# Decoder slots of a four-stage megakernel: scan tail, centring product, squares and mean in two halves of 256 columns

## The reference, cut to what matters

```python
h = jnp.einsum('blv,dv->bld', x, Win) + bin            # x: (32, 64, 512), D = 64
def body(h, p):                                        # 4 layers
    y = silu(layernorm(h, l1w, l1b))                   # first norm
    y = sconv(y, pr + 1j*pi, lr + 1j*li)               # complex exponential filter along time
    h = h + y * scl
    y = layernorm(h, l2w, l2b)                         # second norm
    y = silu(jnp.einsum('bld,fd->blf', y, w1) + b1_)   # F = 256
    y = jnp.einsum('blf,df->bld', y, w2) + b2_
    return (h + y, None)
...
x = _layernorm(x + attn(x)); x = _layernorm(x + xattn(x, ctx, ctx)); x = _layernorm(x + ffn(x))
```

## Time and profile before

| | us |
|---|---|
| median of 3 runs | 315.83 |
| the runs | 313.68, 315.85, 315.83 |
| time of the profiled execution | 316.37 |
| span of the profiled execution | 314.4 |

### The profile page before, as it was taken

How to read it: one execution, slowest core, us unless ns; L and a number is a source line. 1 busy time by engine, 2 the same in 40 slices (tenths; PEclk the granted TensorE clock), 3 DMA queues, 4 the chain that set the end, 5 groups by cost and what they waited for, 6 DMA issues and landing times.

```text
span 314.4 us, 4410 instructions
## 1 busy us (share of the span) xinstructions
PE 271.2 (86%) x1051; PEld 109.0 (35%) x1058; DVE 267.8 (85%) x871; ACT 234.2 (74%) x540; POOL 152.5 (48%) x195
## 2 busy tenths in 40 slices
PE   1587789889898898798999999999999999879762
PEld 1223123223222232244454443544534444423220
DVE  5979799898898987339999999999999999996580
ACT  7046579798898898897478867889788897775642
POOL 1026424014023121302237766787778988899731
PEclk9999799999999999999999999999999999997978
DMA  6999989802021300610000101001112101211141
GB/s 196 394 243 342 379 161 197 180 34 57 11 69 33 133 0 0 111 24 2 3 0 0 18 17 20 18 15 37 51 51 50 40 25 40 53 51 50 50 151 67
DMA packets 22575, 26.52 MB, mean 84 GB/s; under 512 B 10771, under 2 KB 11411, under 8 KB 22550
## 3 DMA queue, kind: packets, MB, share of 16 engines
q1 hardware_dynamic: 20470, 22.06, 22.9%
q0 software_dynamic: 2080, 4.19, 7.9%
HBM read 15.89 MB, written 4.19 MB: 64 GB/s over the span
## 4 chain that ended last, share of the span: by engine, by line
PE 35%; DVE 27%; issue 15%; ACT 14%; DMA 4%; POOL 2%; SPq 1%; POOLq 0%; DVEq 0%; ACTq 0%
PE ps L443 4%; DMA big<-in_xT_dram 4%; DVE ps L1171 4%; PE ps L495 4%; PE ps L469 3%; PE ps L477 3%; PE ps L488 3%; DVE X L1103 3%; DVE big L1183 2%; PE ps L417 2%; PE ps L393 2%; PE ps L430 2%; PE ps L564 2%; ACT L754 2%; DVE ps L1077 2%
## 5 line engine op out<-in xcount | busy, mean ns | idle before, releaser
L1103 DVE SCALAR_TENSOR_TENSOR X<-ps,X 128x512 f32<-128x512 f32 x48 | 32.0, 681 | 11.6 <-PE ps L417 6.3
L651 ACT ACTIVATE big<-X,lnv 128x512 f32<-128x512 f32 x48 | 34.3, 714 | 8.8 <-DVE X L1103 8.7
L393 PE MATMUL ps<-ctx_ring,consts 64*128 64x512 f32 (+1 forms) x96 | 36.5, 659 | 0.0
L443 PEld LDWEIGHTS ps<-consts,big 96*128 96x128 f32 x256 | 29.8, 191 | 13.0 <-issue 10.6
L443 PE MATMUL ps<-consts,big 96*128 96x64 f32 x256 | 32.0, 278 | 0.7 <-DVE big L1138 0.7
L1183 DVE TENSOR_TENSOR big<-ps,ctxf 128x512 f32<-128x512 f32 x48 | 30.3, 682 | 1.3 <-PE ps L477 0.7
L679 ACT ACTIVATE X<-X,lnv 128x512 f32<-128x512 f32 x32 | 25.9, 808 | 0.6
L1171 DVE MATCH_REPLACE8 ps<-m,big 128x64 f32<-128x64 f32 x128 | 25.2, 215 | 0.0
L722 ACT ACTIVATE big<-ps 128x512 f32<-128x512 f32 x16 | 9.5, 596 | 20.9 <-PE ps L457 20.9
L841 POOL TENSOR_TENSOR big<-big 128x512 f32<-128x512 f32 x4 | 5.8, 1444 | 36.0 <-DVE big L1250 26.0
L488 PE MATMUL ps<-big,consts 128*128 128x512 f32 x32 | 17.1, 615 | 5.0 <-DVE qs L1078 4.9
(11 more groups left out here) (185 smaller groups left out, 643.9 us busy)
## 6 DMA issues: line engine op xcount, KB each, us to landing
big<-in_xT_dram SPq DMA_DIRECT2D x4, 1024.0 KB, 9.1
ctx_ring<-in_ctx_dram SPq DMA_DIRECT2D x16, 256.0 KB, 4.2
out_dram<-X SPq DMA_DIRECT2D x16, 256.0 KB, 2.2
X<-in_x_dram SPq DMA_DIRECT2D x2, 1536.0 KB, 11.6
X<-rows_sb POOLq DMA_DIRECT2D x1, 3072.0 KB, 21.7
X<-in_wq_dram SPq DMA_DIRECT2D x1, 1024.0 KB, 5.7
X<-in_x_dram SPq DMA_DIRECT2D x2, 512.0 KB, 4.0
X<-rows_sb POOLq DMA_DIRECT2D x1, 1024.0 KB, 8.6
```

What stands on the lines that cost most here:

```text
L393: mm(bank(LANE_BANK[lane]), mat((CY_0, CY_1, CY_C)[f])[half, :], ctx_ring[half, r * N:(r + 1) * N], start=True, stop=True).then_inc(s_cfor ...
L443: last = mm(ps[:, 2 * N + j * P + b * L:2 * N + j * P + (b + 1) * L], PQ[0:EVEN, b * N + j * P:b * N + (j + 1) * P], mat(IC_E)[0:EVEN, 0:L ...
L651: squared[k, n] = chain(a(JUNK[k], row(n), ACT.Square, bias=st[:, 0:1], scale=-float(V), accum_out=st[:, 2:3]))
L1103: stt(row(m), bank(b), 0.0, row(m), ALU.add, ALU.add, accum_out=st[:, 0:1]).then_inc(s_sum[k], 1)
```

## The change

Three things change, all inside the slots.

1. The tail of the recurrence on DVE: instead of one table product over 1024 columns and one sum over 512, there are for each half h (4 of the 8 sequences, 256 columns of `U1` and of `U2`) a table product over 2 x 256 columns and a sum over 256. Each sum raises `s_scan`.
2. The centring product on PE, the squares of set o on ACT and the variance product of set o on PE are each issued as two instructions of 256 columns. The centring product of half h waits for sum h; both halves of the squares wait for both centring products (`s_xc` at 2m); the variance product of half h waits for the squares of half h; the logarithm that follows waits for both.
3. Order. On ACT the two squares now stand between the logarithm and the exponential of set s, and the second context copy stands before that logarithm. On PE the context form that stood behind the centring product now stands at the slot's beginning, ahead of the variance product of set s.

The core of the diff:

```diff
                 if second:
+                    context_rest(2 * m - 1)
                     pe.wait_ge(s_sq1, m + 1)
                     mm(bank(0), mat(MEAN), SQ[s], start=True, stop=True).then_inc(s_var1, 1)
-                    pe.wait_ge(s_scan, m)
-                    mm(XC[o], mat(CENTER), U1, start=False, stop=False, skip_group_check=True).then_inc(s_xc, 1)
-                    context_rest(2 * m - 1)
+                    for h in range(2):
+                        pe.wait_ge(s_scan, 2 * m - 1 + h)
+                        mm(XC[o][:, half(h)], mat(CENTER), U1[:, half(h)], start=False, stop=False,
+                           skip_group_check=True).then_inc(s_xc, 1)
                     if m == 1:
                         pe.wait_ge(s_b1sum, 1)
-                    pe.wait_ge(s_sq2, m)
-                    mm(bank(2), mat(MEAN), SQ[o], start=True, stop=True).then_inc(s_var2, 1)
+                    for h in range(2):
+                        pe.wait_ge(s_sq2, 2 * m - 1 + h)
+                        last = mm(bank(2)[:, half(h)], mat(MEAN), SQ[o][:, half(h)], start=True, stop=True)
+                    last.then_inc(s_var2, 1)
...
                 if second:
                     context_copied(act, copy, 2 * m - 1, 0)
+                    context_copied(act, copy, 2 * m - 1, 2)
                 act.wait_ge(s_var1, m + 1)
-                chain.then_wait(a(RS[s], bank(0), ACT.Ln, bias=eps[:, :]))
+                logarithm = chain(a(RS[s], bank(0), ACT.Ln, bias=eps[:, :]))
+                if second:
+                    for h in range(2):
+                        act.wait_ge(s_xc, 2 * m)
+                        a(SQ[o][:, half(h)], XC[o][:, half(h)], ACT.Square, bias=base[:, l:l + 1]).then_inc(s_sq2, 1)
+                chain.wait(logarithm)
                 a(RS[s], RS[s], ACT.Exp, scale=-0.5).then_inc(s_rs1, 1)
                 if second:
-                    act.wait_ge(s_xc, m)
-                    a(SQ[o], XC[o], ACT.Square, bias=base[:, l:l + 1]).then_inc(s_sq2, 1)
-                    context_copied(act, copy, 2 * m - 1, 2)
                     act.wait_ge(s_var2, m)
...
-                    do(tt(US, US, tables(l, T_COSG, L), ALU.mult))
-                    tt(U1, U1, U2, ALU.add).then_inc(s_scan, 1)
+                    for h in range(2):
+                        part_of = slice(h * SEQ // 4, (h + 1) * SEQ // 4)
+                        do(tt(US[:, :, part_of, :], US[:, :, part_of, :], half_tables(l, T_COSG, L), ALU.mult))
+                        c = half(h)
+                        tt(U1[:, c], U1[:, c], U2[:, c], ALU.add).then_inc(s_scan, 1)
```

More of the change, by code:

```diff
@@ L282, in stats, with half @@
             return lnv[:, (SETS * k + n % SETS) * 8:(SETS * k + n % SETS + 1) * 8]
+        def half(h):
+            return slice(h * N // 2, (h + 1) * N // 2)
         def here(n):
@@ L1097, in tables, with half_tables @@
                         .broadcast_to([P, 2, SEQ // 2, n]))
+            def half_tables(l, at, n):
+                at += l * T_LEN
+                return (tab[:, at:at + 2 * n].rearrange("p (v t) -> p v t", v=2).unsqueeze(2)
+                        .broadcast_to([P, 2, SEQ // 4, n]))
             VS, US = (piece(k, 2).rearrange("p (v s t) -> p v s t", v=2, t=L) for k in (4, 6))
```

## The result

The changed kernel takes 320.1 us (median of 4 runs, 319.66 to 320.61) against 315.67 for the kernel before on the same chip (313.68 to 315.85): ratio 1.015, 95% interval 1.012 to 1.019. A second set of runs on another occasion gave 320.11 against 315.41, ratio 1.018, 1.014 to 1.022. The forecast was 319.4, range 316.6 to 323.2, slower by over 1% as the likeliest outcome.

The account below looks back on a forecast made before the run. Two rings within a microsecond of each other, through ACT and through DVE, were taken to bound each slot. Slots 2 to 7 +3.58, slot 1 +0.25, slot 8 -0.28 give +3.55 us: 319.4 against 315.83, range 316.6 to 323.2.

Parts of the forecast that it names:

- four DVE instructions start at T+: Recurrence tail on DVE, T being the recurrence's start: two products and two sums, together 0.25 us more DVE work per slot.
- slot 8, second norm's scaling at: Last slot: second norm's scaling comes 10.38 us after the recurrence's start instead of 10.66, so 0.28 us is gained.
- The ring through DVE: DVE's loop from the exponential through its queue to the next recurrence: grows to 13.24 us in even, 13.07 in odd slots.
- The step that decided: Exponential of set s on ACT, now behind the squares: the first norm's scaling on DVE starts 1.29 us late.
- Sizes of the halves: Half instructions on PE and ACT: 0.69 us for a centring half, 0.47 for a square of 256 columns.
- halves don't halve: Rival: centring halves take 1.12 us and squares 0.60 each, 0.87 more per slot; 324.6 us, or 322 at half; chance 0.11.
- The ACT ring: ACT's loop through squares and logarithm: 0.47 us shorter, 12.02, gain lost; rival that it decides: 312.7 us, chance 0.06.
- Behind a weight copy: Slots 4, 6 and 8: a late logarithm of set s on ACT pushes the squares by 0.11 us.
- Two copies and on: DVE from the second norm's scaling over two copies to the next recurrence: 1.95 us when packed.
- Slot 1, the term that was mis-sized: Slot 1, bound by DVE's own list: the tail's 0.25 us goes straight through, +0.25.
- the clock as a rival for later slots: Rival: PE's idle time before the W1 products lowers its clock in every slot; 322 to 331 us, chance 0.05.
- the moved form free: Context form on PE, moved into idle time before the variance of set s: streams 0.86 us, costs nothing.

Follow-up runs that it names:

- e2: Kernel before with one edit: on ACT the exponential of set s stands behind the full-width squares of set o; 319.04 us, 1.011 of the kernel before.
- e3: Changed kernel with the exponential of set s between the two half squares; 318.65 us, 1.011 of the kernel before.
- e1: Changed kernel with the exponential of set s back ahead of the two squares on ACT; 315.04 us, 0.999 of the kernel before.
- e8: The kernel of e1 with the recurrence's DVE tail full width again; 314.70 us, 0.998 of the kernel before.
- e7: The kernel of e1 with both context pieces back in their old places, so only the halves remain; 312.22 us, 0.991 of the kernel before.
- e6: Kernel before plus two products nobody reads, in PE's idle stretch of slot 1; 315.11 us, 1.001 of the kernel before.
- e9: Changed kernel with the context form of slot 1 alone back in its old place; 318.36 us, 1.014 of the kernel before.
- e10: The kernel of e7 plus two unread products on PE in slot 1 ahead of the variance halves; 313.36 us, 0.995 of the kernel before.

## Why the prediction was right, point by point

| step | forecast | measured |
|---|---|---|
| four DVE instructions start at T+ | 3.91, 4.63, 4.97, 5.69 | 3.92, 4.64, 4.99, 5.71 |
| first square starts | 6.90 | 6.92 |
| exponential | 7.66 | 7.65 |
| first norm's scaling on DVE | 8.40 | 8.38 |
| second norm's scaling, even slot | 11.29 | 11.26 |
| next recurrence, even and odd | 13.24, 13.07 | 13.12, 12.98 |
| the same, slots 4 and 6 | 13.35 | 13.45 |
| slots 2 to 7 together | +3.58 | +3.40 |
| slot 8, second norm's scaling at | 10.38 | 10.50 |
| slot 1 | +0.25 | +1.14 |

*The ring through DVE.* The step that decided holds as written: the exponential sits behind squares that can't start sooner, everything queued behind L1265 is pushed, and DVE has no more slack to absorb it. e2 shows the order alone does it, e3 that it goes one to one, e1 that without it the halves gain.

*Sizes of the halves.* The groups of the changed kernel by line and shape:

```profile
L1296 DVE TENSOR_TENSOR big<-big 128x256 f32<-128x256 f32 x16 | 7.1, 445 | 0.6
...
L757 ACT ACTIVATE big<-ps,base 128x256 f32<-128x256 f32 x16 | 6.7, 471 | 3.7 <-PE ps L564 3.7
```

471 ns for a square of 256 columns, 0.47 forecast. The estimate of 0.49 from the Trainium skill, "ScalarE: Activation LUTs", section "What ACT_TABLE_LOAD costs", was a little high. The centring half lasted 0.70 for 0.69. Splitting costs what the fixed parts add and no more, so "halves don't halve" falls. The Trainium skill, "VectorE: DVE Perf Modes", section "The TRN2 errata — SBUF-src ops pay a fixed extra latency per instruction", advises tiles of 512 elements or more. The trace agrees that smaller ones cost DVE time: the tail takes 2.13 us for 1.87 (47.11 - 44.98, and 46.07 - 44.20 before). e8 shows that the work was worth it here, since it let PE start sooner.

*The ACT ring.* It was forecast at 12.02 with its gain lost; e1 shows it at 12.13 to 12.21. In slot 3 of e1 the logarithm starts 8.63 us into the slot where I had 8.52, and the 3.50 behind it hold.

*Behind a weight copy.* Forecast 0.11 us more, measured 0.34: L1265 at T+8.71 to 8.72 in slots 4 and 6. The term had ACT's late logarithm as what pushes the squares, and left out PE's queue. There the variance of set s starts late and the centring halves stand behind it:

```profile
125.30 1.08 PE L561 MATMUL ps<-big,consts 128*128 128x512 f32 x2
126.22 1.03 PE L564 MATMUL ps<-big,consts 128*128 128x256 f32 x4
```

In slot 8 both halves had their sums by 126.16 (the last starts at 125.74 and lasts 0.42) and ran back to back behind L561, until 127.25. ACT had ended its logarithm at 127.11 and waited for PE. In e2, with the same order but no halves, slots 4 and 6 take 13.30.

*Two copies and on.* From L1279 to L1285 took 1.86, not 1.95: instructions that don't wait overlap somewhat more than I packed them. That is most of the 0.1 us by which the periods came out shorter.

*Slot 1, the term that was mis-sized.* "The 0.25 goes straight through" held only in part. Two things were missing. The sums of 256 columns took 0.60 and 0.58 there, not 0.42, while POOL was busy with W1 (the single sum before took 0.85 there for 0.69), so that the tail grew by 0.43 and not 0.25; and PE's clock fell sooner. The stretches of the changed kernel by microsecond, and PE:

```profile
32.00:33.00 1.00, 0.00 (x0) 0.00 (x0) 0.97 (x2) 0.55 (x2) 0.70 (x1) 0.70 1.05 397
33.00:34.00 1.00, 0.00 (x0) 0.00 (x0) 1.00 (x3) 0.00 (x0) 0.00 (x0) 0.50 1.04 381
```

```profile
34.18 2.08 PE L570 MATMUL ps<-big,consts 128*128 128x256 f32 x4 [3.02 <-DVE tab L1260]
36.19 3.63 PE L396 MATMUL ps<-ctx_ring,consts 64*128 64x512 f32 x6
```

Before, the clock was at 1.00 until 35.5 us and at 0.50 until 38.9; now it went to 0.50, 1.2 GHz, at 32.4 us, in the middle of an idle stretch of 3.02 us from which the moved form is missing, and stayed there until 39.2. The variance halves, which had escaped it before, took 2.08 us where the full product had taken 1.13, and the six forms behind them 3.63 (3.84 before). DVE and ACT wait for both; in e2 the low clock lay over work ahead of the variance product and cost nothing. The same two groups in e7:

```profile
33.83 1.13 PE L570 MATMUL ps<-big,consts 128*128 128x256 f32 x4 [2.17 <-DVE tab L1260]
34.89 2.19 PE L396 MATMUL ps<-ctx_ring,consts 64*128 64x512 f32 x6
```

At full clock slot 1 takes 14.78 us in the order before (e6) and 15.18 with halves (e7, e9): so 0.40 of the 1.14 is the halves' and the rest the clock's, which cost 1.46 in the profiled execution of before and 2.20 in that of the changed kernel. I had priced the clock as a rival for later slots, where it stayed at 1.00, and called the moved form free because its new place hides it. But in its old place it kept PE busy. e9 carries this, with the one run in four that went the other way.

*Totals.* Up to L1279 of slot 8 the changed kernel is 4.01 us behind in the profiles: -0.37 (earlier start of the slots), +1.14, +3.40, -0.16. The block pipeline behind takes the same time within 0.2 us, as forecast. So the forecast of +3.55 against a median difference of 4.4 lacks what slot 1 added. That the profiled executions differ by 3.61, all but the forecast, is in part luck: slot 1 was 0.89 over its term and slot 8 0.12, and against them stand 0.18 in slots 2 to 7, 0.37 from the earlier start, 0.21 in the block pipeline and 0.19 around the span; no term of the forecast foresaw the last three.

*What beats both.* e7: halves on DVE, PE and ACT, the exponential ahead of the squares, context pieces left alone; 312.22 us.

## What to carry to other kernels

Where two rings through a loop are nearly as long, cost every edit on both: a wait placed ahead of an instruction on one engine's list delays everything queued behind it on the engine that waits for that instruction. Split a chain into halves to start the next engine sooner, and put what others are waiting for in front of the new wait, not behind it. Work moved into idle time leaves an idle stretch where it was; on TensorE that can cost clock, and the low clock costs time where others wait for the work that falls under it.

## What the runs showed of the hardware that was not expected

In slot 1 TensorE's granted clock fell to 0.50 of full speed behind or within idle stretches no longer than 3.0 us, with PE at work on both sides, and in e6, e7, e9 and e10 it didn't fall there. Whether one program shows both isn't known: each has one trace, and the two of the changed kernel are alike. Every profiled execution has two or three more stretches at 0.50 behind 280 us, in the block pipeline; between 42 and 280 us none has any. The mean clock of a run sums all of them up, so it doesn't tell by itself what happened in slot 1. Of the ten runs of e7 the five at 0.990 or 0.991 took 311.3 to 312.2 us and the five at 0.979 to 0.986 took 312.2 to 314.4; of the kernel before the runs at 0.990 took 313.5 to 314.2 us, those at 0.979 to 0.982 took 314.1 to 317.3. The difference goes with a large part of the spread of all these kernels. The Trainium skill, "TensorE: Matmul & The Clock Gate", section "HAM oscillation — how this bites in real kernels", describes the mechanism, waits that let the clock fall before each new piece of work. The traces agree in part: in slot 1 PE waits for DVE, and the clock falls, but the idle stretch of 1.45 us that comes before the W1 products in slot 2 of the changed kernel leaves it at 1.00. Why filling PE's stretch helped e1 and not the kernel before is open.

A second effect is that a DVE sum of 256 columns lasted 0.60 us beside POOL's work in slot 1 and 0.42 in the later slots. That POOL is the cause was not tested.
